# Issuing the loads of the query and key weights of heads 7 to 63 from GpSimd instead of SyncE

## What is computed

```python
def reference(x, W_Q, W_K, W_V, W_O, b_Q, b_K, b_V, b_O, gate_w, up_w, down_w, gate_s, up_s, down_s):
    xn = _layernorm(x)
    q = einsum('bpd,hde->bphe', xn, W_Q) + b_Q      # k and v alike
    scores = einsum('bqhe,bkhe->bhqk', q, k) / sqrt(128)
    attn = softmax(where(causal, scores, IGNORE))
    z = einsum('bkhe,bhqk->bqhe', v, attn)
    s = einsum('bqhe,hed->bqd', z, W_O) + b_O
    u = xn @ up_w.T * up_s
    ffn = ((silu(xn @ gate_w.T * gate_s) * u) @ down_w.T) * down_s
    return x + s * silu(ffn)
```

## Time and profile before

| what | us |
|---|---|
| median of 3 runs | 1093.69 |
| lowest, highest | 1092.30, 1094.23 |
| the profiled execution | 1092.5 |
| its span in the trace | 1090.3 |

### The profile page before, as it was taken

One profiled execution on the slowest core, in us unless ns is written; L12 is line 12 of the kernel. 1 busy time (PEld: TensorE's weight loads), 2 busy tenths in 40 slices (PEclk: granted clock), 3 DMA queues, 4 the chain that ended last, 5 costly groups with the idle time before them and its releaser, 6 DMA issues.

```text
span 1090.3 us, 21478 instructions
## 1 busy us (share of the span) xinstructions
PE 1065.0 (98%) x7452; PEld 705.5 (65%) x7452; DVE 811.1 (74%) x2011; ACT 736.6 (68%) x1832; POOL 182.1 (17%) x189
## 2 busy tenths in 40 slices
PE   6999999999999999999999999999999999999997
PEld 3444444446777777777777777777777777777764
DVE  7776867786777777777777777777777777777876
ACT  6855556556677777767777777777766666666662
POOL 1000000002101121222212212231000001144333
PEclk9999999999999999999999999999999999999999
DMA  7436576687778779878886897879567667868775
GB/s 277 140 77 178 150 201 189 181 252 198 164 199 208 184 170 265 173 184 219 225 234 152 215 229 166 225 181 258 150 132 205 144 145 180 230 169 236 201 172 161
DMA packets 318532, 207.66 MB, mean 190 GB/s; under 512 B 251872, under 2 KB 284640, under 8 KB 317920
## 3 DMA queue, kind: packets, MB, share of 16 engines
q1 hardware_dynamic: 295872, 179.64, 66.4%
q10 hardware_dynamic: 19200, 15.73, 4.5%
q0 software_dynamic: 3360, 11.01, 2.8%
HBM read 109.87 MB, written 34.60 MB: 133 GB/s over the span
## 4 chain that ended last, share of the span: by engine, by line
PE 80%; ACT 7%; DVE 6%; DMA 5%; issue 2%; SPq 1%; ACTq 0%; DVEq 0%
PE bank L720 71%; PE bank L898 9%; DMA split_qk<-w_out 2%; DMA split_v<-w_out 1%; ACT arena L1251 1%; ACT w_out L1091 1%; DVE arena L1337 1%; ACT arena L1265 1%; ACT V L1110 1%; DMA XT<-V 1%; DVE w_out L1353 1%; DVE arena L1455 1%; DMA arena<-arena 0%; DVE arena L1398 0%; DMA split_o<-w_out 0%
## 5 line engine op out<-in xcount | busy, mean ns | idle before, releaser
L720 PE MATMUL bank<-XT,arena 128*128 128x256 f16 (+2 forms) x1872 | 311.1, 314 | 2.7 <-DVE arena L1455 1.4
L720 PE MATMUL bank<-arena 128*128 128x512 f16 (+1 forms) x1124 | 269.2, 379 | 0.2 <-issue 0.2
L720 PEld LDWEIGHTS bank<-XT,arena 128*128 128x128 f16 (+1 forms) x1872 | 179.2, 98 | 112.4 <-issue 7.4
L1251 ACT ACTIVATE arena<-bank,neg_max 128x512 f32<-128x512 f32 (+3 forms) x256 | 132.8, 525 | 138.2 <-DVE neg_max L1609 138.1
L720 PE MATMUL bank<-ST,arena 128*128 128x256 f16 x1536 | 199.5, 273 | 1.3 <-DVE arena L1546 0.5
L720 PEld LDWEIGHTS bank<-arena 128*128 128x128 f16 x1124 | 109.8, 98 | 107.3 <-issue 0.4
L720 PEld LDWEIGHTS bank<-ST,arena 128*128 128x128 f16 x1536 | 147.9, 98 | 25.7 <-ACT arena L1206 3.7
L1609 DVE CUSTOM_DVE_ANT_0 bank<-bank,mask 128x512 f32<-128x512 f32 (+3 forms) x256 | 118.0, 516 | 20.9 <-PE bank L720 20.6
L1626 DVE SCALAR_TENSOR_TENSOR arena<-arena,inv_sum 128x512 f16<-128x512 f32 (+3 forms) x256 | 127.1, 559 | 8.0 <-ACT arena L1265 6.0
L1265 ACT ACTIVATE arena<-arena,inv_sum 128x512 f16<-128x512 f32 (+3 forms) x256 | 122.3, 557 | 0.0
L898 PE MATMUL bank<-arena,V 128*128 128x512 f16 x756 | 113.3, 299 | 1.5 <-issue 0.9
(11 more groups left out here) (123 smaller groups left out, 1549.1 us busy)
## 6 DMA issues: line engine op xcount, KB each, us to landing
arena<-split_qk SPq DMA_DIRECT2D x64, 896.0 KB, 5.2
w_in<-attn_w_dram SPq DMA_DIRECT2D x64, 256.0 KB, 4.0
split_qk<-w_out ACTq DMA_DIRECT2D x28, 256.0 KB, 3.7
arena<-ffn_w_dram SPq DMA_DIRECT2D x8, 768.0 KB, 4.4
arena<-x_dram SPq DMA_DIRECT2D x20, 256.0 KB, 3.9
parked_silu<-arena ACTq DMA_DIRECT2D x4, 1024.0 KB, 4.7
arena<-split_o SPq DMA_DIRECT2D x4, 1024.0 KB, 6.2
split_qk<-w_out SPq DMA_DIRECT2D x13, 256.0 KB, 3.6
```

The source lines that it names most:

```text
L720: mm = nc.tensor.matmul(out, stationary(a, k), moving(b, k), start=first and n == 0 and i == 0, stop=last and n == len(tiles) - 1 and i == ...
L1251: e = nc.scalar.activation(probs[:, at:at + width], SC[b_][:, col:col + width], ACT.Exp, bias=neg_max[:, i:i + 1], scale=-1.0, accum_out=r ...
```

## The change

The loads of heads 0 to 6 stay with SyncE. From head 7 on GpSimd issues them: `load_qk(u + 3)` inside its `keys_done(u)`, after the wait for the keys' low half of unit u (which product 3 of head u + 1 precedes) and ahead of whatever GpSimd does in that unit. The units 40 to 48, in which GpSimd had nothing to do, get a `keys_done` each for this. The loads have a semaphore of their own, on which TensorE waits from head 7 on, and each waits for the one before it to have landed. Buffers, data, sizes and all arithmetic stay.

```diff
+FIRST_POOL_LOAD = LAG + 2
@@ block.sync
             for u in range(NU):
-                if u + 2 < NU:
+                if u + 2 < FIRST_POOL_LOAD:
                     sp.wait_ge(p3_mm, u + 1)
                     load_qk(u + 2)
@@ block.gpsimd
+            def load_qk(u):
+
+                done = nth_split(u // (T // P), 2, 0)
+                for b in range(4):
+                    pool.wait_ge(w_stored[b], 16 * OUT_OF[:done].count(b))
+                if u == FIRST_POOL_LOAD:
+                    pool.wait_ge(qk_loaded, 16 * FIRST_POOL_LOAD)
+                else:
+                    pool.wait_ge(qk_loaded_pool, 16 * (u - FIRST_POOL_LOAD))
+                pool.dma_start(qkw_flat[:, u % 2], qk_w[head_of(u)].rearrange("p c k n -> p (c k n)")
+                               ).then_inc(qk_loaded_pool, 16)
+
             def keys_done(u):
                 pool.wait_ge(k_lo, 2 * (u + 2))
+                if FIRST_POOL_LOAD <= u + 3 < NU:
+                    pool.wait_ge(p3_mm, u + 2)
+                    load_qk(u + 3)
@@
-            batch_done(0)
-            load_last(0)
+            for u in range(LAST_SLOT_UNIT + 1, LAST_LOADS[0][0]):
+                keys_done(u)
+                if u == LAST_LOADS[0][0] - 1:
+                    batch_done(0)
+                    load_last(0)
             for u, t in LAST_LOADS:
                 keys_done(u)
                 load_last(t)
@@ block.tensor, unit(u)
-                pe.wait_ge(qk_loaded, 16 * (n + 1))
+                if n < FIRST_POOL_LOAD:
+                    pe.wait_ge(qk_loaded, 16 * (n + 1))
+                else:
+                    pe.wait_ge(qk_loaded_pool, 16 * (n + 1 - FIRST_POOL_LOAD))
```

More of the change, by code:

```diff
@@ L322, in build @@
         qk_loaded = sem("qk_loaded")
+        qk_loaded_pool = sem("qk_loaded_pool")
         wv_loaded = [sem(f"wv_loaded{i}") for i in range(3)]
```

## The result

The changed kernel takes **1149.11 us** (median; 1147.27 to 1152.58) against 1093.53 for the kernel before, a ratio of 1.051, 95% interval 1.0495 to 1.0525. The forecast was 1092.2, between 1089.5 and 1096.0. The profiled execution took 1147.27 us.

A forecast was written before the change was run, and what follows sets the result against it. TensorE was taken to set the pace in attention. Terms of -0.2, -0.96, -1.1, +2.45 and -1.7 summed to -1.5 us, giving a median of 1092.2 us, range 1089.5 to 1096.0.

The forecast's parts named there:

- the issue: GpSimd's issue of the 896 KB load: 0.55 us, starting 0.30 us after T, the end of the keys' low half.
- the landing: The load issued by GpSimd: 6.2 us to land, at T + 6.5, with no wait for the head it brings.
- The removed 57 issues: SyncE without 57 load issues: 0.2 us gained, from units 13 and 29, between 0 and 0.4.
- GpSimd wins in odd units: Odd units 5 to 39: the subtraction behind the issue holds V's low half until T + 2.30; +2.45 us in all.
- the first rival: VectorE wins in odd units, so the +2.45 falls away: -3.9 us, 1089.8; chance 0.18.
- A waiting VectorE operation gets its turn before the next one: Even units 4 to 38: V's low half ends at T + 2.58, whether one or two subtractions follow.
- forecast 0.32: Units 6, 22 and 38: V's low half ends 0.33 us earlier, each gives 0.32 us; -0.96 together.
- the forecast's 0.14 to 0.26: Units 12, 16, 20, 28, 32, 36: TensorE's wait before weighing V shrinks 0.14 to 0.26 us each; -1.1 together.
- The odd units' +2.45: Units 7, 19, 23, 35 and 39: products 6 and 5 lose 0.3 and 0.19 us, five times 0.49.
- rival 4: Late load runs into the next transposes, four to eight units at 0.5 us: +3 us, 1095.2; chance 0.08.
- The tail's -1.7: Units 54, 58 and 60: with three issues GpSimd's addition starts at T + 1.95, when VectorE is through; -1.7 us.
- Rival 3: Issue takes longer than 0.55 us, the subtraction behind it still holds VectorE off: +4.8 us, 1098.5 at 1.0 us; chance 0.12.

## Why the prediction was wrong

- **What bounds the kernel, the issue, the landing: right.** TensorE sets the pace, the issue takes 0.564 us against 0.55, starts at T + 0.30 and puts the first subtraction at T + 0.89 against 0.86. The load lands in 5.2 us, earlier than the estimate of 6.2, and with SyncE as its issuer a late load cost nothing that the median shows.
- **The removed 57 issues: -0.2 forecast, not shown.** In the run with the issue behind the subtractions the late weighings of units 13, 14 and 30 come 0.6 us earlier, and units 37 and 38 are 0.9 longer, so that units 4 to 39 come out at +0.5. But the run with the wait for V's low half gains the same 0.6 with all loads on SyncE, so it can't be put down to the removed issues.
- **GpSimd wins in odd units: right, by a reason that isn't.** Unit 54 had shown it, and the first rival, built on the margin of 0.09 us and the rule of the Trainium skill (SBUF — State Buffer, Who interferes with whom), fell. But from unit 54 I took that GpSimd holds the path before its recorded start, always. Without an issue it doesn't: with four memsets VectorE came 0.16 us first and kept its 0.42. Unit 54 was the effect of the issue already.
- **"A waiting VectorE operation gets its turn before the next one": the step that failed.** It came from unit 7, where the second subtraction is stretched. There no issue stands ahead of the subtractions. The one place in the trace with an issue ahead, unit 54, has a single addition and then a wait, so it couldn't say what a second operation does. I carried a rule from gap-free arithmetic to arithmetic behind an issue, and gave no case of the rule failing a price. That price, 1.1 to 1.25 us for each further operation in V's low half, made some 42 of the +48.5 us of units 4 to 39: so much went when a gap between the operations gave the turn back.
- **With turns, how good were the terms?** The run with a gap between the subtractions is the forecast's own timeline. Its V's low half is 1.59 and 1.38 us against 1.53 and 1.34. Units 7, 23 and 39 gain 0.29 each (forecast 0.32). The units 12, 16, 28 and 32 gain 0.14 to 0.25 each, in the forecast's 0.14 to 0.26; in 20 and 36 that is covered by the odd loss before them. The odd units' +2.45 (five times 0.49) was 3.9 (0.83, 0.70, 0.84, 0.69, 0.83). Three things had no term or were put at nothing: unit 4, where a difference of weights follows the issue and the weighing waits for V's low half (+1.0); units 10 and 26, behind odd units that were to lose nothing (+0.37 each); and 3.8 us of waits for late transposes, of the kind and about the size of rival 4. From unit 4 to unit 40 it is +7.7 where my terms give +0.4. So even with turns the time, 1106.16, lies above my range.
- **The tail's -1.7: right**, at -1.45 (0.38, 0.34, 0.48, 0.25), by the mechanism named; V's low half takes 0.68 us in units 54, 58 and 60.
- **The closing drain was missing.** It is +4.6 us, 0.082 for each of the 57 issues. I had read only the units. The program ends 0.3 us behind that instruction, and its 5 us stood in the trace of before. With this term alone the forecast would have been slower, not level (1096.8).
- **Rival 3 named the right culprit**, the subtraction behind the issue holding VectorE off, but made it depend on the issue's length. The length was as forecast. The rival of late transposes, seen in no weighing of the changed kernel, happened in other runs (up to 2.3 us once), and didn't decide. (Rivals 3 and 4 add up to 0.20; my 0.19 is a slip.)
- The Trainium skill (DMA: Bandwidth & Descriptors, Issuing engines are not separate DMA queues) says that another issuer only saves sequencer time. The trace agrees for the transfer, 5.2 us from either queue. It doesn't for the kernel: 48.5 us by the operations behind the issue and 4.6 by the closing drain.

## What to carry to other kernels

Count an issue moved to GpSimd not by its half microsecond but by the GpSimd arithmetic that follows it without a gap: VectorE operations with two SBUF inputs may be shut out to the end of that run, so put the issue last, or behind it a short operation and a wait for its result. Before such a move look for a row that shows the same sequence, issue and then two or more operations; if there is none, the far end of the range is the whole run, in every unit. And where GpSimd and VectorE share work in each unit of a TensorE-bound loop, a wait that lets the short critical VectorE operation go first may be worth more than any moved load (here 0.4%).

## What was not expected of the hardware

- Behind an issue on GpSimd, its gap-free operations keep a waiting VectorE operation out to the last of them, 5.1 us for four (one unit of 36 escaped in one run, none in the others); a gap of 0.09 us gives the turn back; without an issue it comes after one operation. Why an issue does this isn't shown by any run.
- GpSimd's closing drain grows with the number of its issues, 5.05, 6.77 and 9.7 us with 0, 21 and 57 more, and not with their bytes (9.7 with 57 of 64 KB).
- After TensorE had idled 3.7 us in unit 19, matmuls came at half pace (granted clock 0.50), 0.21 us for 256 columns instead of 0.107, and 1.26 us more went there.
